# Layer-norm statistics moved into the tail of the stage ahead, and another order of four exponentials, in a decoder of twelve stages

## What is computed

```
def _layernorm(x, axis=-1, eps=1e-05):
    m = jnp.mean(x, axis=axis, keepdims=True)
    v = jnp.var(x, axis=axis, keepdims=True)
    return (x - m) / jnp.sqrt(v + eps)
...
    x = x + _L0_attn_ref(_layernorm(x, axis=-1), ...)
    x = x + _L0_xattn_ref(_layernorm(x, axis=-1), ctx_1024, ctx_1024, ...)
    x = x + _L0_ffn_ref(_layernorm(x, axis=-1), ...)
...
```

```
        scores = jnp.einsum('bqhd,bkhd->bhqk', q, k) / jnp.sqrt(jnp.float32(D))
        scores = jnp.where(mask == 0, jnp.float32(-1e+30), scores)
        attn = jax.nn.softmax(scores, axis=-1)
        ctx = jnp.einsum('bhqk,bkhd->bqhd', attn, v).reshape(B, Sq, E)
        return ctx @ Wo + bo
```

## Time and profile before

| | us |
|---|---|
| median of three runs | 1491.03 (1489.07 to 1491.22) |
| profiled execution | 1486.77 |
| its span | 1485.0 |
| mean granted clock of PE over the span | 0.959 |
| busy: PE / DVE / ACT / POOL | 1346.3 / 755.1 / 659.8 / 198.5 |

### The profile page before, as it was taken

One profiled execution on the slowest core, in us unless ns is written; L12 is line 12 of the kernel. 1 busy time (PEld: TensorE's weight loads), 2 busy tenths in 40 slices (PEclk: granted clock), 3 DMA queues, 4 the chain that ended last, 5 costly groups with the idle time before them and its releaser, 6 DMA issues. The chain is left out here.

```text
span 1485.0 us, 31308 instructions
## 1 busy us (share of the span) xinstructions
PE 1346.3 (91%) x12470; PEld 1044.4 (70%) x12470; DVE 755.1 (51%) x1719; ACT 659.8 (44%) x1714; POOL 198.5 (13%) x199
## 2 busy tenths in 40 slices
PE   7999899989989899998999979998994887799898
PEld 6776667776557677787999965678993566577743
DVE  3656677745556577520000266610115587467666
ACT  3444326633357456425444344632232677146440
POOL 3000261000014310050111400040005000310000
PEclk9999999999999999999999997999997999889999
DMA  6000232011401100165999200184402000250100
GB/s 218 1 1 1 56 62 38 4 44 36 87 8 21 33 24 3 57 211 214 346 349 343 63 9 20 32 334 146 153 26 76 0 2 2 56 67 4 49 27 17
DMA packets 44014, 120.20 MB, mean 81 GB/s; under 512 B 12001, under 2 KB 28510, under 8 KB 38482
## 3 DMA queue, kind: packets, MB, share of 16 engines
q1 hardware_dynamic: 33118, 62.04, 14.6%
q0 software_dynamic: 7616, 53.12, 10.3%
q10 hardware_dynamic: 3136, 3.03, 0.7%
HBM read 95.78 MB, written 11.00 MB: 72 GB/s over the span
## 5 line engine op out<-in xcount | busy, mean ns | idle before, releaser
L794 PE MATMUL wide<-early_kt,early_q 32*100 32x361 f32 x512 | 96.3, 490 | 3.3 <-PEq L67 1.5
L2532 ACT ACTIVATE l1f_hidden<-wide,l1f_pack 128x128 f32<-128x128 f32 x160 | 58.7, 367 | 79.7 <-PE wide L2471 70.0
L2688 DVE TENSOR_TENSOR l1f_out<-summed,l1f_pack 128x256 f32<-128x256 f32 x20 | 8.5, 425 | 144.7 <-PE summed L2479 144.7
L2471 PEld LDWEIGHTS wide<-l1f_rt,l1f_pack 128*128 128x128 f32 x640 | 76.2, 196 | 1.7 <-issue 0.8
L2471 PE MATMUL wide<-l1f_rt,l1f_pack 128*128 128x128 f32 x640 | 76.4, 279 | 0.6 <-ACT l1f_rt L2522 0.6
L2479 PE MATMUL summed<-l1f_pack,l1f_hidden 128*128 128x256 f32 x320 | 72.4, 380 | 0.0
L114 PE MATMUL summed<-ident 128*128 128x128 f32 x284 | 38.9, 302 | 31.6 <-PEq L67 31.6
L1204 DVE TENSOR_REDUCE l3x_mx<-wide 100x2 f32<-100x722 f32 x64 | 55.8, 907 | 22.6 <-PE wide L794 22.5
L1204 DVE TENSOR_REDUCE l1x_mx<-wide 100x2 f32<-100x722 f32 x64 | 55.5, 907 | 21.0 <-PE wide L794 21.0
L1204 DVE TENSOR_REDUCE l0x_mx<-wide 100x2 f32<-100x722 f32 x64 | 55.5, 907 | 19.5 <-PE wide L794 19.5
L2479 PEld LDWEIGHTS summed<-l1f_pack,l1f_hidden 128*128 128x128 f32 x320 | 59.4, 191 | 7.1
(11 more groups left out here) (610 smaller groups left out, 3359.5 us busy)
## 6 DMA issues: line engine op xcount, KB each, us to landing
l2f_w<-l2f_w_dram SPq DMA_DIRECT2D x16, 1024.0 KB, 11.2
ctxt<-ctxt_dram SPq DMA_DIRECT2D x4, 1083.0 KB, 17.2
early_kt<-soon_kd SPq DMA_DIRECT2D x32, 90.8 KB, 3.2
l1f_sorted_x<-l1f_zeros SPq DMA_DIRECT2D x4, 640.0 KB
l1f_rows<-l1f_sorted_x SPq DMA_DIRECT2D x20, 128.0 KB, 7.3
l1f_sorted_y<-l1f_out ACTq DMA_DIRECT2D x20, 128.0 KB, 9.1
l0f_w<-l0f_w_dram SPq DMA_DIRECT2D x18, 128.0 KB, 2.1
l1f_shared<-l1f_shared_dram SPq DMA_DIRECT2D x1, 2180.0 KB, 8.4
```

The source lines that it names most:

```text
L794: pe.matmul(wide[0:S, i, 0:SKV], q4[R * i:R * (i + 1), g % 2, b, g // 2, :], kt[R * i:R * (i + 1), g % 2, b, g // 2, 0:SKV], start=True, s ...
L2471: last = pe.matmul(wide[:, f % 4, 0:P], w1_of(w, k, f), rt[:, n % 2, k, :], start=k == 0, stop=k == KC - 1)
L2532: act.activation(hidden[:, f, 0:P], wide[:, f % 4, 0:P], ACT.Gelu, bias=b1_of(pack[:, n % SLOTS, :], f)).then_inc(sem["h_ready"], 1)
L2688: dve.tensor_tensor(out[:, n % 2], summed[:, n % 2, 0:E], b2_of(pack[:, n % SLOTS, :]), ALU.add).then_inc(sem["y_ready"], 1)
```

## The change

It has four parts. (1) The statistics are split by batch (statistics, variances, roots, inverses). In the tail of ten stages DVE, after each addition to net.x, drains and takes that batch's statistics; after batch 3 it combines those of batches 0 to 3 and adds EPS (signal early_var), ACT takes their roots as the last instruction of its list (early_std), and DVE waits for it and inverts as its last step. In l2_attn the first four statistics come together after the first four additions; in l1_ffn ACT's roots come ahead of the last copies. The head of the next stage combines only batches 4 to 7, normalises batches 0 to 3 at once, then waits for the roots of the others, inverts and goes on. (2) The spare products at the head go from 18 to 5 (l0_ffn, l1_ffn, l2_ffn, l3_attn, l3 cross, l3_ffn) and from 12 to 5 (l2_cross); l0 cross keeps its 12, and the five ahead of the quads stay. (3) In the quads ACT takes the exponentials in the order 2, 0, 3, 1, and PE's waits name single exponentials by `exponential(n, j)`. (4) The turn of the maxima becomes four products of 32 columns. The same edits of the tail and head as shown for cross_attn16 and l0_ffn are made in the other stages.

```diff
--- before.py
+++ after.py
-def norm_stats_vector(dve, net, var_ready, std_ready):
-
-    for b in range(B):
-        dve.bn_stats(net.stats[:, b, :], net.x[:, b, :])
+EARLY = B // 2
+
+
+def statistics(dve, net, b):
+    return dve.bn_stats(net.stats[:, b, :], net.x[:, b, :])
+
+
+def variances(dve, net, b0, b1):
     dve.drain()
-    for b in range(B):
+    for b in range(b0, b1):
         dve.bn_aggr(net.moments[:, b, :], net.stats[:, b, :])
     dve.drain()
-    dve.tensor_scalar(net.std[:], net.moments[:, :, 1:2], EPS, None, ALU.add).then_inc(var_ready, 1)
-    dve.wait_ge(std_ready, 1)
-    dve.reciprocal(net.rstd[:], net.std[:])
+    return dve.tensor_scalar(net.std[:, b0:b1], net.moments[:, b0:b1, 1:2], EPS, None, ALU.add)
+
+
+def roots(act, net, b0, b1):
+    return act.activation(net.std[:, b0:b1], net.std[:, b0:b1], ACT.Sqrt)
+
+
+def inverses(dve, net, b0, b1):
+    dve.reciprocal(net.rstd[:, b0:b1], net.std[:, b0:b1])
     dve.drain()
...
@@ cross_attn16
-                    keep_busy(pe, net, 18 if fresh else 12)
+                    keep_busy(pe, net, 5 if fresh else 12)
...
+        def exponential(n, j):
+            if j < 2:
+                return j + 1 if n == 0 else Q * n + 2 * j
+            return Q * (n + 1) + (j - 2) * 2 - 1 if n < QUADS - 1 else Q * (n + 1) + j - Q + 1
...
                 def turn_maxima(n):
                     pe.wait_ge(sem["m_ready"], 2 * n + 2)
                     if n >= 1:
-                        pe.wait_ge(sem["p_ready"], Q * (n - 1) + 1)
-                    pe.transpose(scored[0][:, LOW:LOW + S], mx[:, n % 2, :], net.ident[0:S, 0:S]).then_inc(sem["mt_psum"], 1)
+                        pe.wait_ge(sem["p_ready"], exponential(n - 1, 0))
+                    for i in range(Q):
+                        last = pe.matmul(scored[0][R * i:R * (i + 1), LOW:LOW + S], mx[:, n % 2, R * i:R * (i + 1)], net.ident[0:S, 0:S], start=True, stop=True)
+                    last.then_inc(sem["mt_psum"], 1)
...
                 def score_by_key(n, turns):
...
-                        pe.wait_ge(sem["p_ready"], Q * (n - 1) + turns[-1] + 1)
+                        pe.wait_ge(sem["p_ready"], exponential(n - 1, turns[-1]))
...
                 def weigh(n):
                     b, g = n // NQ, n % NQ
-                    pe.wait_ge(sem["p_ready"], min(Q * (n + 1) + 2, Q * QUADS))
+                    pe.wait_ge(sem["p_ready"], max(exponential(n, Q - 1), exponential(min(n + 1, QUADS - 1), 1)))
...
                 for n in range(QUADS + 2):
                     if 1 <= n <= QUADS:
-                        exps(n - 1, (2, 3))
+                        exps(n - 1, 2)
                     if n < QUADS:
-                        exps(n, (0,))
+                        exps(n, 0)
+                    if 1 <= n <= QUADS:
+                        exps(n - 1, 3)
                     if n >= 2:
                         take(n - 2)
                     if n < QUADS:
-                        exps(n, (1,))
+                        exps(n, 1)
                 for b in range(B):
                     copy_yt(b)
+                act.wait_ge(sem["early_var"], 1)
+                roots(act, net, 0, EARLY).then_inc(sem["early_std"], 1)
...
                 if not spread:
-                    for b in range(B):
-                        dve.bn_stats(net.stats[:, b, :], net.x[:, b, :])
-                    dve.drain()
...
+                    variances(dve, net, EARLY, B).then_inc(sem["var_ready"], 1)
...
                     for b in range(B):
+                        if b == EARLY:
+                            dve.wait_ge(sem["std_ready"], 1)
+                            inverses(dve, net, EARLY, B)
                         normalise(dve, net, xn[:, b, :], b).then_inc(sem["xn_ready"], 1)
...
                     if b >= 3:
                         add(b - 3)
+                    dve.drain()
                     if b < B:
-                        dve.drain()
                         divide(b)
+                    if b >= 3:
+                        statistics(dve, net, b - 3)
+                        if b - 3 == EARLY - 1:
+                            variances(dve, net, 0, EARLY).then_inc(sem["early_var"], 1)
+                dve.wait_ge(sem["early_std"], 1)
+                inverses(dve, net, 0, EARLY)
                 dve.drain()
...
@@ l0_ffn
-                keep_busy(pe, net, 18)
+                keep_busy(pe, net, 5)
...
                         dve.scalar_tensor_tensor(out=net.x[:, b, :], in0=banks[n % YB], scalar=combine[:, e, b:b + 1],
                                                  in1=net.x[:, b, :], op0=ALU.mult, op1=ALU.add).then_inc(sem["y_added"], 1)
-                    dve.drain()
+                        if e == NEX - 1:
+                            dve.drain()
+                            statistics(dve, net, b)
+                            if b == EARLY - 1:
+                                variances(dve, net, 0, EARLY).then_inc(sem["early_var"], 1)
+                    dve.drain()
+                dve.wait_ge(sem["early_std"], 1)
+                inverses(dve, net, 0, EARLY)
+                dve.drain()
...
```

More of the change, by code:

```diff
@@ L1661, in _ @@
                     activate(e)
+                act.wait_ge(sem["early_var"], 1)
+                roots(act, net, 0, EARLY).then_inc(sem["early_std"], 1)
             @block.vector
             def _(dve):
-                norm_stats_vector(dve, net, sem["var_ready"], sem["std_ready"])
+                variances(dve, net, EARLY, B).then_inc(sem["var_ready"], 1)
                 for b in range(B):
+                    if b == EARLY:
+                        dve.wait_ge(sem["std_ready"], 1)
+                        inverses(dve, net, EARLY, B)
                     if b >= 2:
@@ L2690, in _ @@
                     add_experts(b)
-                    statistics(b)
+                    statistics(dve, net, b)
                 for u in range(LATE, UNITS - 1):
@@ L2829, in add @@
                     dve.tensor_tensor(net.x[:, b, :], net.x[:, b, :], summed[0:S, b % 2, 0:E], ALU.add).then_inc(sem["zt_added"], 1)
+                variances(dve, net, EARLY, B).then_inc(sem["var_ready"], 1)
                 for b in range(B):
-                    dve.bn_aggr(net.moments[:, b, :], net.stats[:, b, :])
-                dve.drain()
-                dve.tensor_scalar(net.std[:], net.moments[:, :, 1:2], EPS, None, ALU.add).then_inc(sem["var_ready"], 1)
-                dve.wait_ge(sem["std_ready"], 1)
-                dve.reciprocal(net.rstd[:], net.std[:])
-                dve.drain()
-                for b in range(B):
+                    if b == EARLY:
+                        dve.wait_ge(sem["std_ready"], 1)
+                        inverses(dve, net, EARLY, B)
                     normalise(dve, net, xn[:, b, :], b).then_inc(sem["xn_ready"], 1)
@@ L2855, in _ @@
                             add(b)
+                        dve.drain()
+                        for b in range(HALF):
+                            statistics(dve, net, b)
+                        variances(dve, net, 0, EARLY).then_inc(sem["early_var"], 1)
                 for b in range(HALF, B):
                     add(b)
+                    dve.drain()
+                    statistics(dve, net, b)
+                dve.wait_ge(sem["early_std"], 1)
+                inverses(dve, net, 0, EARLY)
                 dve.drain()
@@ L3649, in _ @@
                     dve.tensor_tensor(net.x[:, t, :], net.x[:, t, :], wide[0:S, t % 4, 0:E], ALU.add).then_inc(sem["out_done"], 1)
+                    dve.drain()
+                    statistics(dve, net, t)
+                    if t == EARLY - 1:
+                        variances(dve, net, 0, EARLY).then_inc(sem["early_var"], 1)
+                dve.wait_ge(sem["early_std"], 1)
+                inverses(dve, net, 0, EARLY)
                 dve.drain()
```

106 lines of the change are left out of this document (64 added, 42 removed).

## The result

The changed kernel takes **1503.2 us** (median of four runs, 1501.72 to 1506.05) against 1490.05 for the kernel before beside it: ratio 1.0104, 95% interval 1.0076 to 1.0132 (ratios here and below are estimates from the runs of both sides; the quotient of these two medians is 1.0088). Ratios and means leave out the two runs, one of ten_spares and one of tail_spares, that were over 1.5% above the fastest of their kernel. Forecast were 1482.9 us, in a range of 1472 to 1495, and a gain. The kernel became slower by about as much as the third rival said, but for the most part not by its mechanism.

The account below looks back on a forecast made before the run. PE, busy 91% of the span, was taken as the bound, so only its waits counted. Heads -20.4, tails +14.3, quads -4 and clock +2 gave -8.1: from 1491.0 to 1482.9 us, range 1472 to 1495.

Parts of the forecast that it names:

- third rival: Clock falls in the heads; five of ten lead to half-clock stretches costing 21 us, time 1502; chance 0.14.
- Quads: Loop of quads in three cross stages: new order and turn gain 0.045 us a quad, -4 us (0 to -9).
- ring: Circle of waits between PE and ACT in each quad of the cross stages: 2.42 us new against 2.46.
- second rival: Quads give the whole idle time ahead of the turn, 0.2 to 0.28 us each, some 1465; chance 0.07.
- Heads: Stage starts: fewer statistics on DVE before the first normalised batch, at most 3.5 us each, together -20.4 us.
- Tails: Stage ends: added drains, statistics, variances and reciprocals on DVE, together +14.3 us.
- l0_ffn's 4.6 us: Tail of l0_ffn: back-to-back additions leave statistics bare, 3.8 us, with variances and reciprocal 4.6 us.
- l2_attn's 1.8 - 0.5: In l2_attn the tail costs 1.8 us and the head gives back 0.5.
- Clock: Fewer spare products and longer tails: half of one more half-clock stretch, +2 us (bounds -4 to +17).
- -6.1 + 2: Heads and tails together, -6.1 us, plus the clock's +2.

Follow-up runs that it names:

- ten_spares: quads_back with GpSimd's first memsets of l3_attn and l3 cross late, no statistics in l0_ffn's tail, ten spare products at seven heads instead of five: ratio 0.9971.
- tail_spares: quads_back with GpSimd's first memsets of l3_attn and l3 cross late, no statistics in l0_ffn's tail, and spare products added in idle tails: ratio 0.9990.
- quads_back: The changed kernel with the old order of exponentials and one transpose for the maxima again: ratio 1.0028 to the kernel before.

## Why the prediction was wrong

**Quads: the step that failed** (forecast -4, measured +11 us; 93 times 0.10 is 9.5, and l3 cross lost more by its two waits). Three terms were wrong. First, I let exponential 0's scores be there 0.07 us before it started in the kernel before. It starts 0.19 us after the end of the last product of its scores there, and 0.22 after it in the new order, where ACT stands idle for it; I had put 0.15, by the other pair. So there was nothing to gain from an earlier place. Second, I let the moved exponential 3 end at 238.70, 0.13 us ahead of its user, and left out that 0.11 us pass from an exponential's end to PE's load (241.84 to 241.95); the margin was none, and the order costs 0.06 us. Third, I bounded the turn by the passes of the weighing, 0.17 to 0.28 us, without the pause behind them ahead of the scores (0.15); it is 0.34, a cost of 0.10 a quad where my bound was 0.05. The rows had all three: the pause ahead of the scores stood in the trace of before, and so did each time from the end of an exponential to the instruction that waited for it. I took a ring apart whose slack was below 0.1 us with latencies rounded to that size.

The second rival was wrong too: the idle time ahead of the turn stayed at 0.28 to 0.29 us when the turn got the weighing's shape. By the Trainium skill, "TensorEngine Tiling (Array Packing)", Key Properties, a change of the tiling mode drains the engine; the traces are in keeping with it only in that the pause behind the turn, ahead of the scores, is there in both shapes (0.10 and 0.15 us). Ahead of the turn no drain can be seen beside the wait for the exponential, whose end (246.78) is 0.11 us before the turn's load.

PE's wait of 4.73 us for "issue" in l3 cross was in no rival. One quad of 6 to 9 us stands in that place in all four profiles with products in the turn, and none over 4.3 us in those with the transpose; a fetch of instructions (16 KB, 1.7 to 1.8 us) comes behind a burst of DMAs at its time. In these four PE stops between 1.7 us before and 0.1 us after the fetch begins, and goes on 1.3 to 1.7 us after it has ended. A fetch as long stands in the kernels with the transpose too (1317.34 in the kernel before), and PE goes on beside it. That PE ran out of instructions is argued from this, not shown by a run that moves the fetch alone.

**Heads** (forecast -20.4). The mechanism was right where nothing else stood in the way: in l3_ffn PE turns the first batch 1.2 us after the start instead of 4.7, the third 2.7 instead of 5.7, and the stage is 3.0 us shorter (forecast 3.1). PE in the timelines, before and after:

```profile
1407.91 0.72 PE L3706 MATMUL turned<-ident,l3f_xn 100*128 100x100 f32 x4 [0.45 <-DVE l3f_xn L107]
1408.93 0.36 PE L3706 MATMUL turned<-ident,l3f_xn 100*128 100x100 f32 x2 [0.29 <-DVE l3f_xn L107]
```

```profile
1422.32 0.57 PE L3800 MATMUL turned<-ident,l3f_xn 100*128 100x100 f32 x4
1423.84 0.36 PE L3800 MATMUL turned<-ident,l3f_xn 100*128 100x100 f32 x2 [0.95 <-ACT l3f_xt L3868]
```

The chain of waits after shows what came next, ACT's table for the exponentials. In the kernel before it was loaded from 1407.15 to 1408.43, beside the normalising and turning of the first batches, and PE waited for DVE; now PE waits 0.95 us for the copy behind it:

```profile
1421.84 0.20 ACT std L102
1422.05 0.02 issue
1422.07 1.28 ACT L3864
1423.35 0.01 issue
1423.36 0.35 ACT l3f_xt L3868
```

In l3_attn and l3 cross the term was wrong by 2.4 and 1.8 us: GpSimd's memsets took the place of the statistics. I looked at what PE needs next and not at what DVE's first instructions share with GpSimd, though both memsets stood in the trace of before at that time. The Trainium skill, "SBUF — State Buffer", Who interferes with whom, says that tensor_scalar can enter a mode in which it shares a port pair with GpSimd, which one of the two holds for a whole instruction. The traces agree: 2.56 us beside the memset, 0.17 without it, and statistics unhurt (eight in 2.71 us beside the memset of 3.08, before). That section would have told me in advance where to look.

**Tails** (forecast +14.3). The largest term, l0_ffn's 4.6 us, was measured as 8.0 - 3.4 = 4.6 (without the reciprocal), and l2_attn's 1.8 - 0.5 as 1.3. What the sum lacked is what the longer tail does to PE: 5.37 us idle, and 2.6 us more for the key projections behind it.

**Clock** (forecast +2, bounds -4 to +17). Taking away 85 products costs 13 us where nothing else is changed; in the changed kernel shorter heads make up for part, and half clock grew by 24 us in the profiles, by 33 in the mean of the runs (129 to 162), 5 to 7 us at 0.2 each. The third rival's mechanism is real, and its price was smaller than I had put it. The Trainium skill, "TensorE: Matmul & The Clock Gate", Part 4: PE-mode transpose, has transposes not count as busy for the clock. No run here shows it. The starts of l1_ffn and l2_ffn run at 0.51 for 14 us in the stretches above, but they are not mostly transposes, as I had it for the heads: these stand in pairs of 0.57 us between products of eight columns (0.72 us) and ahead of wide ones (128x200, 128x361). The clock fell at 634.3 and 968.8, 0.7 us after PE had begun again behind 2.3 and 2.0 us of idle time, when it was still at its spare products and had turned nothing; and it rose again, at 647.9 and 982.4, while the wide products ran. An added product a batch changed nothing there. Heads and tails together, without the quads, came to +0.28% (4 us, quads_back), where I had -6.1 + 2. The memsets (4 by the traces) and the clock (172 us at half clock in the mean of its ten runs, some 8 us at 0.2) are more than the difference; how it divides between them isn't shown.

## What to carry to other kernels

In a ring whose steps are tenths of a us apart, reckon each wait with its own measured latency and ask for the second-latest input of every step before moving an instruction: here the moved exponential was the next wait. Work that looks spare may be what holds the clock or keeps two engines apart; before it is shortened or moved, look at what else runs in that stretch on the engine's neighbours, and put filler where the engine is idle anyway: it held the clock there, though the gain in time is not settled. Statistics belong in a tail only where it waits for something: in a tail that is bound by their own engine they are paid in full.

## What the runs showed of the hardware

A float32 product with the identity is no cheap transpose: from its first load to the next scores 0.39 us as one of 128 columns, 0.34 as four of 32, 0.24 as a transpose. DVE's sum of four numbers took 2.56 us beside a GpSimd memset and 0.17 without. And identity products move the half clock in one and the same network, in the mean of the runs: 129 us to 194 where 85 were taken from the heads, 162 to 123 where they were put back, 147 to 125 where five became ten, 150 to 125 where 54 went into idle tails. A profiled execution alone was up to 40 us off such a mean (tail_spares, 93 against 132).
